# An attention and FFN block on one core: four groups of narrow value products, issued in two places or in four

## The chip, the cores and the metric

The program runs on one core of a Trainium2 chip. The metric is the device time of one execution in microseconds (us). The kernel before takes 776.32 us (median of 3 runs, 775.79 to 776.37).

The names of the engines in the profile: PE is the matrix engine (TensorE), PEld its weight loads, DVE the vector engine, ACT the scalar engine, POOL the GpSimd, SP the engine that issues most DMAs.

## What is computed

The input x has 16 sequences of 256 tokens and 256 features; the context has the same shape. First an mLSTM style attention of 8 heads of 32 features (queries from the normalised x, keys and values both the context), then a feed-forward network with two hidden layers of 1024.

```
x = x + mlstm(layernorm(x), ctx, ctx)          # gates, running maxima, 8 heads
#   s_mat  = (q @ k.T / sqrt(32)) * exp(log_d - max(log_d))
#   h      = (s_mat @ v) / (max(|rowsum(s_mat)|, exp(-m)) + 5e-5), then rms norm and gain
u = layernorm(x)
h = silu((u @ w1.T) * s1) * ((u @ w2.T) * s2)  # 256 -> 1024, twice
h = gelu((h @ h1.T) * t1)                      # 1024 -> 1024
h = gelu((h @ h2.T) * t2)                      # 1024 -> 1024
x = x + (h @ w3.T) * s3                        # 1024 -> 256
```

## The kernel before

The 16 sequences are worked in 8 pairs of two (`PAIRS`, index i). A pair's 512 tokens are the moving side of the FFN's matmuls; features lie on partitions. Every FFN operand is held as a high part and a low part, so each product is two matmuls, one of `h_hi` and one of `h_lo`, both into one PSUM bank of `ps_f` (L1434 and L1435 in the first layer, L1468 and L1469 in the hidden layers, L1503 and L1504 in the last). A matmul with 512 moving columns of this kind is called a large one below.

The engines work a software pipeline that is written out by hand. While PE runs the FFN of pair i, it also runs, at fixed places between the FFN's matmuls, the attention of pair j = i + 1 and the first steps (transposes, gates) of pair g = i + 2. Each engine has one list of instructions in the order in which they are written, and semaphores tie the lists together. PE's list for one pair is written by `batch`:

- `swiglu` for m of 0 to 7 (8 large matmuls each), with `scores(j, 0)` after m = 4;
- `hidden_layer(i, 0, ...)`, the first hidden layer. It runs the output groups m = 0 and 1 side by side over k = 0 to 6, calling `between(k)` after each k (4 large matmuls), then k = 7 for both. Each later m is 8 large matmuls, a call of `within(m)`, 8 large matmuls, a call of `after(m)`. The hooks `after_2`, `within_2` and `between_2` hang on it. `scores(j, 1)` comes after m = 3, `make_state(j)` after m = 5;
- `hidden_layer(i, 1, ...)`, the second hidden layer, with `between_3`, `within_3` and `after_3`: `turn_z(g)` after k = 3, `gates(g)` after m = 2, `turn_z2(j)` and `turn_rows(g)` after m = 7;
- `project`, the last layer.

`values(j, t, b)` is the step in question: sequence b of the pair, token tile t (each of the two 128-token tiles). It multiplies the weighted scores (held in `decay`) by the values (`v_aug`). The weights of one such matmul are 128 rows by 32 columns, so a head's 128 tokens are done as 4 strips of 32 (`values_of_head`), and a call has 8 heads times 4 strips = 32 matmuls of 33 moving columns, into bank 2 + b of `ps_a`. Each of them has two records in the trace. Such matmuls are called narrow ones below. `make_state` (L1371) has 16 of the same kind; `scores` (L1356) has 16 with 32 rows of weights; `read_state` (L1407) has 4 with the full 128 by 128.

What hangs on the values: after tile 0 of both sequences ACT copies them to `num` (`take_near`, L656, placed in ACT's list behind the group m = 5 of the first hidden layer), and only then may tile 1 be written to the same banks (`s_near`). After tile 1 of both, DVE adds the far part (`take_num`, L955, placed in DVE's list behind the last low part of the first hidden layer, L1076), and goes on from there through the division, the rms norm, the residual and the second layer norm. DVE's list then leads to the gates' scans of pair g, whose last step (L894) PE waits for in `turn_rows` (L1336). SP's load of the next values (L341) waits for the last values group too.

The pair after next uses the same code; there are 7 pairs i with an attention stage.

Of the kernel before, what the change touches and what calls it, by code (L numbers as in the profile page):

```python
# [73 lines left out]
def build(nc, x, ctx_tok, ctx_t, gate_w, gate_b, outnorm_w, w_cols, scales, w3_s, out):  # L74
    with ExitStack() as stack:
# [167 lines left out]
        def first(j):  # L243
            return isinstance(j, int) and j == 0
# [61 lines left out]
        def weights_in(eng, layer):  # L306
            eng.wait_ge(s_wgt[layer], 16 * sum(n == layer for n, _ in LOADS))
# [934 lines left out]
        def _(pe):  # L1242
# [6 lines left out]
            def turn_z(j):  # L1249
                pe.wait_ge(s_z, j)  # L1250

                if j >= 2:
                    pe.wait_ge(s_num, j)
                else:
                    pe.wait_ge(s_far, j)
                turn(z, ps_a[:, 0:CH], s_zT)
# [10 lines left out]
            def turn_z2(j):  # L1267
                pe.wait_ge(s_z2, j)
                if isinstance(j, int) and 0 < j < PAIRS - 1:

                    pe.wait_ge(s_zhi, j)
                turn(z2, ps_a[:, 0:CH], s_z2T)
# [60 lines left out]
            def turn_rows(j):  # L1333
                pe.wait_ge(s_scan, SCAN_STEPS * j + SCAN_STEPS)
                for t in range(TILES):
                    last = pe.transpose(rows_out[:, t * ROWS:(t + 1) * ROWS], rows[:, t * P:(t + 1) * P], ident[0:ROWS, 0:ROWS])  # L1336
                last.then_inc(s_colT, 1)

            def scores(j, b):
                if b == 0:  # L1340

                    pe.wait_ge(s_zTe, j + 1)
                    pe.wait_ge(s_cols, j + 1)
                    reuse(pe, s_z2lo, j)
                    reuse(pe, s_num, j)
                elif first(j):
                    pe.wait_ge(s_exp, EXP_STEPS)
                else:
                    pe.wait_ge(s_smat, SMAT_STEPS * j + ROWGRP)
                for t in range(TILES):  # L1350
                    for c in range(CH):
                        for r in range(ROWGRP):
                            d = slice(r * DH, (r + 1) * DH)
                            col = (c * TILES + t) * P
                            at = slice((b * TILES + t) * P, (b * TILES + t + 1) * P)
                            last = pe.matmul(score_out(j, b, r)[:, col:col + P], ctxT(j)[d, c, at], zT(j)[d, c, at], start=True, stop=True)  # L1356
                last.then_inc(s_qk, 1)

            def make_state(j):
                pe.wait_ge(s_kwt, j + 1)  # L1360
                pe.wait_ge(s_smat, SMAT_STEPS * j + (ROWGRP if first(j) else SMAT_STEPS))
                for b in range(W):
                    if first(j):
                        for c in range(CH):
                            h = slice(c * ROWGRP, (c + 1) * ROWGRP)
                            last = pe.matmul(ps_a[:, b, c * ROWGRP * DV:(c + 1) * ROWGRP * DV], k_wt[:, b, h, :],
                                             v_aug[:, b * TILES, h, :], start=True, stop=True)
                        continue
                    for h in range(HEADS):
                        strip = slice(h % ROWGRP * DH, (h % ROWGRP + 1) * DH)  # L1370
                        last = pe.matmul(ps_a[strip, b, h * DV:(h + 1) * DV], k_wt[:, b, h, :],  # L1371
                                         v_aug[:, b * TILES, h, :], start=True, stop=True)
                last.then_inc(s_st, 1)

            def values_of_head(j, b, h, t):

                for n in range(STRIPS):
                    strip = slice(n * STRIP, (n + 1) * STRIP)
                    last = pe.matmul(value_out(j, b, t)[strip, h * DV:(h + 1) * DV], decay_of(b, h, t)[:, strip],  # L1379
                                     v_aug[:, b * TILES + t, h, :], start=True, stop=True)  # L1380
                return last
# [11 lines left out]
            def values(j, t, b):  # L1393
                if t == 1:

                    pe.wait_ge(s_near, j + 1)
                for h in range(HEADS):
                    last = values_of_head(j, b, h, t)
                last.then_inc(s_pv, 1)
# [21 lines left out]
            def swiglu(i, m, as_is):  # L1421
                bank = (turn_of(i) + 2 * m) % 4
                if m == 1:

                    reuse(pe, s_ysc, W * i)
                if m >= 2:
                    pe.wait_ge(s_hf, KH * i + m - 1)
                per = KH // N_W1
                for half, base in enumerate((UNIT_W1, UNIT_W2)):
                    if as_is and m % per == 0:  # L1430
                        pe.wait_ge(*unit_landed(i - PAIRS, base + m // per))
                    for c in range(CH):
                        w = columns(base + m // per, (m % per * CH + c) * P, P, as_is)
                        pe.matmul(ps_f[:, bank + half], w, moving(z2_hi[:, c], as_is), start=(c == 0), stop=False)  # L1434
                        last = pe.matmul(ps_f[:, bank + half], w, moving(z2_lo[:, c], as_is), start=False, stop=(c == CH - 1))  # L1435
                last.then_inc(s_ab, 1)

            def first_swiglu():

                for part, landed in ((z2_hi, (s_z2hi_first, s_z2hi)), (z2_lo, (s_z2lo_first, s_z2lo))):  # L1440
                    for c in range(CH):
                        pe.wait_ge(landed[c], 1)
                        for half, base in enumerate((UNIT_W1, UNIT_W2)):
                            last = pe.matmul(ps_f[:, half], columns(base, c * P, P, False), part[:, c],
                                             start=(part is z2_hi and c == 0), stop=(part is z2_lo and c == CH - 1))
                last.then_inc(s_ab, 1)
# [75 lines left out]
            def count_inexact():  # L1522

                pe.wait_ge(s_inexact_sum, 1)
                pe.matmul(ps_a[0:1, 0, 0:1], inexact_sum[:], ones[:], start=True, stop=True).then_inc(s_inexact_all, 1)

            def batch(i, a_stage, g_stage, as_is=False, last=False):
                j, g = i + 1, i + 2
                if as_is:
                    pe.wait_ge(s_y, W * i)  # L1530
                weights_in(pe, 0)
                if not first(i):
                    pe.wait_ge(s_z2lo, i + 1)
                if first(i):
                    first_swiglu()
                for m in range(1 if first(i) else 0, KH):
                    swiglu(i, m, as_is)
                    if first(i) and m == 2:
                        turn_rows(1)
                    if a_stage and m == 4:  # L1540
                        scores(j, 0)

                def after_2(m):
                    if a_stage and m == 3:
                        scores(j, 1)
                    if a_stage and m == 5:
                        make_state(j)
                        values(j, 0, 0)
                        values(j, 0, 1)

                def after_3(m):
                    if g_stage and m == 2:
                        gates(g)
                    if a_stage and m == 7:
                        turn_z2(j)
                    if g_stage and m == 7:
                        turn_rows(g)

                def within_2(m):
                    if a_stage and m == 7:  # L1560
                        read_state(j)
                        values(j, 1, 0)
                        values(j, 1, 1)

                def between_2(k):
                    pass

                def between_3(k):
                    if g_stage and k == 3:
                        turn_z(g)  # L1570

                def within_3(m):
                    pass

                weights_in(pe, 1)
                hidden_layer(i, 0, as_is, between_2, within_2, after_2)
                weights_in(pe, 2)
                hidden_layer(i, 1, as_is, between_3, within_3, after_3)
                weights_in(pe, 3)
                project(i, as_is, last)  # L1580
                if last:
                    count_inexact()
# [97 lines left out]
```

## Time and profile before

| | |
|---|---|
| median of 3 runs | 776.32 us |
| the profiled execution | 775.79 us |
| its span, first to last instruction | 773.9 us |
| mean granted clock of TensorE | 0.996 |
| PE busy | 764.5 us |
| DVE busy | 545.8 us |
| ACT busy | 381.6 us |
| POOL busy | 50.9 us |

The span and the engines' times are of one profiled execution. Between the span and that execution's own time lie 1.9 us. A busy share says how long an engine had an instruction under way; large matmuls overlap, so the distance between the starts of two of them is shorter than the duration of one.

### The profile page before, as it was taken

How to read it: one execution, taken by the hardware profiler on the slowest of the kernel's cores; microseconds unless marked ns; L12 is line 12 of the kernel's file. 1: busy time of each engine (PE TensorE's matmuls, PEld its weight loads, DVE VectorE, ACT ScalarE, POOL GpSimd, SP SyncE). 2: the span in 40 equal slices, each digit the busy share in tenths (PEclk: the TensorE clock that was granted, in tenths of full speed). 3: DMA queues.
4: the chain of work that ended last, by engine and by line, in shares of the span. 5: the costliest groups of instructions: out<-in, count | busy, mean ns of one | idle time of the engine just before them, and what ended most of it. 6: DMA issues, size and time to landing. Idle time of an engine off the chain costs nothing.

```text
span 773.9 us, 14930 instructions
## 1 busy us (share of the span) xinstructions
PE 764.5 (99%) x6170; PEld 640.6 (83%) x6170; DVE 545.8 (71%) x1294; ACT 381.6 (49%) x570; POOL 50.9 (7%) x63
## 2 busy tenths in 40 slices
PE   8999999999999999999999999999999999999997
PEld 7878888878888888878888888888889788888886
DVE  6787867586856969578675877758695684965544
ACT  3455645464554733556445564636435562445331
POOL 3300020000200011000200002000020000000000
PEclk9999999999999999999999999999999999999999
DMA  8933010501122000320005000130102100541540
GB/s 338 368 124 115 29 30 28 191 1 35 52 100 92 28 30 27 122 71 29 30 28 189 2 30 29 69 151 9 50 29 110 54 1 3 185 142 29 162 137 29
DMA packets 14615, 63.43 MB, mean 82 GB/s; under 512 B 2016, under 2 KB 2896, under 8 KB 11728
## 3 DMA queue, kind: packets, MB, share of 16 engines
q1 hardware_dynamic: 12960, 50.12, 18.7%
q0 software_dynamic: 1296, 11.53, 3.8%
q8 instruction: 49, 0.80, 0.4%
q10 hardware_dynamic: 288, 0.79, 0.3%
q14 instruction: 22, 0.18, 0.1%
HBM read 53.94 MB, written 8.50 MB: 81 GB/s over the span
## 4 chain that ended last, share of the span: by engine, by line
PE 85%; DVE 11%; ACT 2%; issue 1%; POOL 0%; POOLq 0%; DVEq 0%; ACTq 0%
PE ps_f L1468 24%; PE ps_f L1469 23%; DVE decay L917 8%; PE ps_f L1434 8%; PE ps_f L1435 7%; PE ps_f L1503 4%; PE ps_f L1504 4%; PE ps_a L1356 2%; PE ps_a L1379 2%; DVE decay L933 2%; PE ps_a L1246 2%; PE ps_f L1587 1%; PE ps_a L1282 1%; PE ps_f L1302 1%; PE ps_a L1407 1%
## 5 line engine op out<-in xcount | busy, mean ns | idle before, releaser
L1468 PE MATMUL ps_f<-h_hi,wgt 128*128 128x512 f32 x1024 | 401.7, 392 | 0.0
L1469 PE MATMUL ps_f<-h_lo,wgt 128*128 128x512 f32 x1024 | 398.8, 389 | 0.0
L1468 PEld LDWEIGHTS ps_f<-h_hi,wgt 128*128 128x128 f32 x1024 | 192.2, 188 | 41.6 <-issue 0.6
L1469 PEld LDWEIGHTS ps_f<-h_lo,wgt 128*128 128x128 f32 x1024 | 192.3, 188 | 38.8
L691 ACT ACTIVATE work<-ps_f,scl 128x512 f32<-128x512 f32 x128 | 87.5, 684 | 161.2 <-PE ps_f L1469 160.6
L1076 DVE TENSOR_TENSOR h_lo<-work,h_hi 128x512 fp32r<-128x512 f32 x128 | 86.5, 689 | 98.2 <-ACT h_hi L696 97.1
L1434 PE MATMUL ps_f<-h_hi,wgt 128*128 128x512 f32 x252 | 99.8, 396 | 0.0
L1435 PE MATMUL ps_f<-h_lo,wgt 128*128 128x512 f32 x252 | 98.7, 392 | 0.0
L678 ACT ACTIVATE work<-ps_f,scl 128x512 f32<-128x512 f32 x64 | 44.1, 689 | 98.2 <-PE ps_f L1435 96.3
L696 ACT ACTIVATE h_hi<-work 128x512 fp32r<-128x512 f32 x128 | 81.0, 633 | 4.1
L1067 DVE SCALAR_TENSOR_TENSOR work<-ps_f,scl,work 128x512 f32<-128x512 f32 x64 | 48.0, 750 | 47.0 <-ACT work L678 47.0
L917 DVE SCALAR_TENSOR_TENSOR decay<-decay,cols,future 128x128 f32<-128x128 f32 x224 | 64.5, 362 | 0.0
L1503 PE MATMUL ps_f<-wgt,h_hi 128*128 128x256 f32 x256 | 62.3, 285 | 0.0
L1504 PE MATMUL ps_f<-wgt,h_lo 128*128 128x256 f32 x256 | 61.7, 283 | 0.0
L1434 PEld LDWEIGHTS ps_f<-h_hi,wgt 128*128 128x128 f32 x252 | 47.3, 188 | 14.7 <-DVE work L1067 3.8
L1435 PEld LDWEIGHTS ps_f<-h_lo,wgt 128*128 128x128 f32 x252 | 47.4, 188 | 8.6
L1504 PEld LDWEIGHTS ps_f<-wgt,h_lo 128*128 128x128 f32 x256 | 49.1, 192 | 0.0
L1503 PEld LDWEIGHTS ps_f<-wgt,h_hi 128*128 128x128 f32 x256 | 49.0, 192 | 0.0
L621 ACT ACTIVATE decay<-decay 128x1024 f32<-128x1024 f32 x28 | 29.7, 1061 | 35.3 <-DVE decay L917 35.3
L1072 DVE TENSOR_TENSOR h_lo<-work,h_hi 128x512 fp32r<-128x512 f32 x64 | 43.7, 682 | 0.8
L682 ACT ACTIVATE h_hi<-work 128x512 fp32r<-128x512 f32 x64 | 39.9, 623 | 2.4 <-DVE work L1067 2.4
L933 DVE SCALAR_TENSOR_TENSOR decay<-ps_a,decay 128x512 f32<-128x512 f32 x60 | 37.1, 677 | 0.7 <-PE ps_a L1356 0.7
(195 smaller groups left out, 701.1 us busy)
## 6 DMA issues: line engine op xcount, KB each, us to landing
decay<-m_rows SPq DMA_DIRECT2D x14, 1024.0 KB, 6.1
decay<-w_cols SPq DMA_DIRECT2D x22, 512.0 KB, 4.2
wgt<-w_cols POOLq DMA_DIRECT2D x5, 1024.0 KB, 11.8
v_aug<-ctx_tok SPq DMA_DIRECT2D x8, 528.0 KB, 4.0
wgt<-w_cols POOLq DMA_DIRECT2D x2, 2048.0 KB, 14.4
x_kept<-xs SPq DMA_DIRECT2D x8, 512.0 KB, 2.6
xs<-x SPq DMA_DIRECT2D x7, 512.0 KB, 3.6
ctxT<-ctx_t SPq DMA_DIRECT2D x7, 512.0 KB, 3.3
```

The costliest lines, as they stand in the source:

```text
L691: act.activation(work[:, m % GELU], ps_f[:, (turn_of(i) + m) % 4], ACT.Gelu, scale=scl[:, 2 + layer, m:m + 1]).then_inc(s_gelu, 1)
L696: act.activation(h_hi[1 - layer][:, m], work[:, m % GELU], ACT.Copy).then_inc(s_hi, 1)
L917: last = dve.scalar_tensor_tensor(part, part, cols[:, t, row:row + 1], future[:], ALU.subtract, ALU.add)
L933: dve.scalar_tensor_tensor(s, score_out(j, b, r).rearrange("p (c n) -> p c n", c=CH), SCORE_SCALE, s, ALU.mult, ALU.mult)\
L1067: dve.scalar_tensor_tensor(work[:, 2 + m % 2], ps_f[:, bank], scl[:, 1, m:m + 1], work[:, m % 2], ALU.mult, ALU.mult).then_inc(s_hf, 1)
L1076: dve.tensor_tensor(h_lo[1 - layer][:, m], work[:, m % GELU], h_hi[1 - layer][:, m].bitcast(F32), ALU.subtract).then_inc(s_lo, 1)
L1434: pe.matmul(ps_f[:, bank + half], w, moving(z2_hi[:, c], as_is), start=(c == 0), stop=False)
L1435: last = pe.matmul(ps_f[:, bank + half], w, moving(z2_lo[:, c], as_is), start=False, stop=(c == CH - 1))
L1468: pe.matmul(ps_f[:, bank], w, moving(h_hi[layer][:, k], as_is), start=(k == 0), stop=False)
L1469: last = pe.matmul(ps_f[:, bank], w, moving(h_lo[layer][:, k], as_is), start=False, stop=(k == KH - 1))
L1503: pe.matmul(to, moving(h_hi[0][:, k, q * P:(q + 1) * P], as_is), w, start=(k == 0), stop=False)
L1504: last = pe.matmul(to, moving(h_lo[0][:, k, q * P:(q + 1) * P], as_is), w, start=False, stop=(k == KH - 1))
```

## The change

Two of the four calls of `values` for a pair move. `values(j, 0, 1)` goes from directly behind `values(j, 0, 0)` to 8 large matmuls later, the middle of the group m = 6. `values(j, 1, 1)` goes from directly behind `values(j, 1, 0)` to behind the remaining 8 large matmuls of m = 7 and the first 4 of the second hidden layer. No instruction is added or taken away, and the lists of DVE, ACT, POOL and SP stay as they are.

```diff
                     if a_stage and m == 5:
                         make_state(j)
                         values(j, 0, 0)
-                        values(j, 0, 1)
...
                 def within_2(m):
+                    if a_stage and m == 6:
+                        values(j, 0, 1)
                     if a_stage and m == 7:
                         read_state(j)
                         values(j, 1, 0)
-                        values(j, 1, 1)
...
                 def between_3(k):
+                    if a_stage and k == 0:
+                        values(j, 1, 1)
                     if g_stage and k == 3:
                         turn_z(g)
```

PE's list behind the group m = 5 of the first hidden layer, before. Rows are line, operation, result and operands, tile size, a count, and the semaphores waited for.

```order
L1371 MATMUL ps_a<-v_aug,num 32x33 [waits s_smat,s_kwt]
L1371 MATMUL ps_a<-v_aug,num 32x33 x15
L1379 MATMUL ps_a<-v_aug,decay 32x33 x64
L1468 MATMUL ps_f<-h_hi,wgt 128x512 [waits s_gelu]
L1469 MATMUL ps_f<-h_lo,wgt 128x512
```

The same place with the change:

```order
L1371 MATMUL ps_a<-v_aug,num 32x33 x15
L1379 MATMUL ps_a<-v_aug,decay 32x33 x32
L1468 MATMUL ps_f<-h_hi,wgt 128x512 [waits s_gelu]
L1469 MATMUL ps_f<-h_lo,wgt 128x512
L1468 MATMUL ps_f<-h_hi,wgt 128x512
L1469 MATMUL ps_f<-h_lo,wgt 128x512
L1468 MATMUL ps_f<-h_hi,wgt 128x512
L1469 MATMUL ps_f<-h_lo,wgt 128x512
L1468 MATMUL ps_f<-h_hi,wgt 128x512
L1469 MATMUL ps_f<-h_lo,wgt 128x512
L1379 MATMUL ps_a<-v_aug,decay 32x33 x32
L1468 MATMUL ps_f<-h_hi,wgt 128x512
```

The 64 narrow matmuls of tile 0 now stand as 32 and 32, with 8 large ones between them.

PE's list in the middle of the group m = 7, before; the second hidden layer begins behind 8 large matmuls, at the row that waits for `s_lo`, `s_gelu` and `s_wgt2`:

```order
L1407 MATMUL ps_a<-state,zT 128x132 x3
L1379 MATMUL ps_a<-v_aug,decay 32x33 [waits s_near]
L1379 MATMUL ps_a<-v_aug,decay 32x33 x31
L1379 MATMUL ps_a<-v_aug,decay 32x33 [waits s_near]
L1379 MATMUL ps_a<-v_aug,decay 32x33 x31
L1468 MATMUL ps_f<-h_hi,wgt 128x512
L1469 MATMUL ps_f<-h_lo,wgt 128x512
```

With the change, the end of the first hidden layer and the start of the second:

```order
L1469 MATMUL ps_f<-h_lo,wgt 128x512
L1468 MATMUL ps_f<-h_hi,wgt 128x512 [waits s_lo,s_gelu,s_wgt2]
L1469 MATMUL ps_f<-h_lo,wgt 128x512
L1468 MATMUL ps_f<-h_hi,wgt 128x512 [waits s_lo,s_gelu]
L1469 MATMUL ps_f<-h_lo,wgt 128x512
L1379 MATMUL ps_a<-v_aug,decay 32x33 [waits s_near]
L1379 MATMUL ps_a<-v_aug,decay 32x33 x31
L1468 MATMUL ps_f<-h_hi,wgt 128x512 [waits s_lo]
```

Tile 1 of the second sequence now runs inside the second hidden layer, behind that layer's first 4 large matmuls.

## Rows read from the trace of the kernel before

**Rows 1.** The page: busy time of each engine, and the granted clock by slice.

```profile
PE 764.5 (99%) x6170; PEld 640.6 (83%) x6170; DVE 545.8 (71%) x1294; ACT 381.6 (49%) x570; POOL 50.9 (7%) x63
...
PEclk9999999999999999999999999999999999999999
```

**Rows 2.** Busy time by window, one pair: busy, records, clock, DMA share, GB/s.

```profile
191.00:282.00 91.00, 90.90 (x777) 76.28 (x765) 66.39 (x161) 47.61 (x69) 6.23 (x4) 1.00 0.17 59
```

**Rows 3.** Timeline of PE behind m = 5: start us, length us, line, shapes, count.

```profile
273.28 0.39 PE L1469 MATMUL ps_f<-h_lo,wgt 128*128 128x512 f32 x1
273.60 0.46 PE L1371 MATMUL ps_a<-v_aug,num 128*32 128x33 f32 x32
273.88 1.34 PE L1379 MATMUL ps_a<-v_aug,decay 128*32 128x33 f32 x128
275.15 0.50 PE L1468 MATMUL ps_f<-h_hi,wgt 128*128 128x512 f32 x1
275.48 0.39 PE L1469 MATMUL ps_f<-h_lo,wgt 128*128 128x512 f32 x1
...
276.87 0.39 PE L1469 MATMUL ps_f<-h_lo,wgt 128*128 128x512 f32 x1
```

**Rows 4.** Timeline of PE in the middle of m = 7, same pair.

```profile
280.50 0.39 PE L1469 MATMUL ps_f<-h_lo,wgt 128*128 128x512 f32 x1
280.72 1.06 PE L1407 MATMUL ps_a<-state,zT 128*128 128x132 f32 x8
281.71 1.32 PE L1379 MATMUL ps_a<-v_aug,decay 128*32 128x33 f32 x128
282.97 0.50 PE L1468 MATMUL ps_f<-h_hi,wgt 128*128 128x512 f32 x1
283.30 0.40 PE L1469 MATMUL ps_f<-h_lo,wgt 128*128 128x512 f32 x1
...
285.61 0.39 PE L1469 MATMUL ps_f<-h_lo,wgt 128*128 128x512 f32 x1
```

**Rows 5.** All narrow matmuls of the values: duration ns min/median/max, starts.

```profile
L1379 PE MATMUL ps_a<-v_aug,decay x1792: 192/197/218, 91.4 to 647.9; 128*32 128x33 f32 x200
```

**Rows 6.** Timeline of PE around the first scores of a pair.

```profile
243.19 0.39 PE L1435 MATMUL ps_f<-h_lo,wgt 128*128 128x512 f32 x1
243.51 1.17 PE L1356 MATMUL ps_a<-zT,ctxT 32*128 32x128 f32 x32
244.61 0.50 PE L1434 MATMUL ps_f<-h_hi,wgt 128*128 128x512 f32 x1
244.95 0.40 PE L1435 MATMUL ps_f<-h_lo,wgt 128*128 128x512 f32 x1
```

**Rows 7.** Timeline of PE around the transposes of `turn_z`.

```profile
288.56 1.03 PE L1246 MATMUL ps_a<-ident,z 128*128 128x128 f32 x8
289.35 0.48 PE L1468 MATMUL ps_f<-h_hi,wgt 128*128 128x512 f32 x1
289.67 0.40 PE L1469 MATMUL ps_f<-h_lo,wgt 128*128 128x512 f32 x1
```

**Rows 8.** Timelines of DVE and ACT: the takers of the values.

```profile
286.51 0.69 DVE L1076 TENSOR_TENSOR h_lo<-work,h_hi 128x512 fp32r<-128x512 f32 x1 [3.98 <-ACT h_hi L696]
287.12 0.70 DVE L955 TENSOR_TENSOR num<-ps_a,state 128x528 f32<-128x528 f32 x1
...
275.25 0.61 ACT L656 ACTIVATE num<-ps_a 128x528 f32<-128x528 f32 x1 [0.19 <-PE ps_a L1379]
```

**Rows 9.** Timelines of DVE and PE: scans' end, and `turn_rows`.

```profile
316.43 0.27 DVE L894 TENSOR_SCALAR rows<-state 16x128 f32<-16x128 f32 x1
...
317.60 0.30 PE L1336 MATMUL ps_a<-ident,rows 80*128 80x80 f32 x2
```

**Rows 10.** Waits of PE's weight loads: us in total, times, longest.

```profile
PEld ps_a L1356 <- DVE decay L933: 3.7, 7, 0.5
```

## The prediction

> **What bounds the kernel now.** I read the busy times first: PE has work under way for 764.5 of 773.9 us, DVE for 545.8, ACT for 381.6, and every slice of the granted clock shows a 9, the top digit [rows 1]. Then a window of one pair: 90.90 of 91.00 us busy at a granted clock of 1.00, that is 2.4 GHz, with the DMA engines at 0.17 [rows 2]. So from the first pair to the last PE's own list sets the end: what PE's stream gains or loses in length, the kernel gains or loses, unless a wait appears. The only wait on another engine that returns in every pair is at the second scores, 3.7 us over 7 times [rows 10]; its cause, the masks on DVE, starts from the first FFN layer of the same pair, which the change does not touch, so it moves along with PE.
>
> Busy shares don't tell what a change of order costs, since matmuls overlap. That is read from the starts of neighbouring matmuls on the timeline. Undisturbed large ones are 0.227 us apart: from 276.87 [rows 3] to 280.50 [rows 4] there are 16 distances in 3.63 us.
>
> **What a run of narrow matmuls costs at its edges.** At the first place [rows 3]:
> - Entry: from the start of the last large matmul, 273.28, to the first narrow one, 273.60, is 0.32 us and not 0.227: 0.09 more.
> - Exit: the run of 128 records ends at 273.88 + 1.34 = 275.22; one of them takes 0.197 [rows 5], so the last one starts at 275.02, and the large one behind it at 275.15: 0.13. Within the run the starts are (275.02 - 273.88) / 127 = 0.009 apart, so 0.12 is due to the exit.
> - Aftermath: the first large matmul lasts 0.50, its neighbour starts 0.33 behind it, and the 8th large one starts at 276.87. Seven distances take 1.72 us where 7 x 0.227 = 1.59: 0.13 more.
>
> Together 0.09 + 0.12 + 0.13 = 0.34 us at the edges of a run, whatever is in it. At the second place [rows 4] the aftermath over the 12 large matmuls from 282.97 to 285.61 is 2.64 - 11 x 0.227 = 0.14, and the exit from 281.71 + 1.32 - 0.197 = 282.83 to 282.97 is 0.14 - 0.01 = 0.13; with an entry of 0.09, 0.36 us. Are these edges of a size that depends on the length of the run? The scores, a run of 32 records, show the same three signs [rows 6]: 0.32 from 243.19 to 243.51, 0.50 for the first large one, 0.34 to the next. So a run a quarter as long pays the same.
>
> **The change, part by part.** Nothing is added or removed: the 896 narrow matmuls of the values stand in the new list too, with their 1.1 to 1.3 us per 128 records. What changes is the number of runs. Before, a pair has two runs with values in them; now it has four. The first run keeps the state and 64 records, then come 8 large matmuls, then 64 records on their own; the second keeps the read of the state and 64 records, then 12 large ones, then 64 records. In 8 large matmuls the aftermath of [rows 3] is over (from 276.87 on the distances are 0.227), so neither new piece shares its edges with the old. Each new run costs one full set of edges:
>
> 2 runs x 7 pairs x 0.35 us (the mean of 0.34 and 0.36) = 4.9 us. The start of a fresh run looks a little quicker than its middle (32 records of the state in 0.28 us [rows 3], 8.8 ns each, against 9.0), a gain of 64 x 0.2 ns = 0.01 per run: 0.1 us. The sum is 4.8 us.
>
> What hides it? Nothing that I find: PE has no slack to lay it in. What other engines do with the moved times:
> - ACT copies tile 0 at 275.25, as soon as the last narrow one is done [rows 8]. The last narrow matmul of tile 0 comes later by the 8 large ones plus one set of edges, 1.8 + 0.34 = 2.2 us, so the copy lies at about 277.4 to 278.0. Its reader on PE starts at 281.71 [rows 4]: over 3 us of cover. Queued behind the copy on ACT is the group m = 6, which PE ends 8 large matmuls (1.8 us) after the values, later than a copy of 0.61 us: nobody waits for it.
> - DVE takes the values of tile 1 at 287.12, directly behind the last low part [rows 8]. The last large matmul of m = 7 starts 64 records sooner against its run (0.57 us) and one set of edges later, so this low part and `take_num` come about 0.23 sooner, at 286.9. The values of tile 1 then lie behind the 4th large matmul of the next layer. Before, that layer began 8 large ones behind 282.97 with the aftermath, at 284.93 (282.97 + 8 x 0.227 + 0.14); now it begins at 284.93 - 0.57 + 0.34 = 284.70, the run starts 3 x 0.227 + 0.32 later, at 285.70, its last record starts at 286.26 and ends at 286.46. DVE would be there at 286.9: 0.4 us to spare. This is the closest call of the change.
> - SP's load of the next values waits for the last narrow matmul, which comes some 3.4 us later. Its reader is in the next pair's stretch, and behind it in SP's list stands a wait for the residual of the same pair, which comes later still. Cost: nothing.
>
> **A rule of the skill.** The trace shows the entry and exit gaps of 0.09 and 0.12 where the weights go from 128 columns to 32 and back [rows 3], and none at the entry of the read of the state, whose weights are as wide as the large ones': 280.50 to 280.72 is the usual distance [rows 4]. The Trainium skill, page "TensorEngine Tiling (Array Packing)", section "Key Properties", says that changing the tiling mode, not just the tile, drains the engine, which speaks against this change. By that rule alone each new run has two drains and no aftermath, and the sum would be 14 x (0.09 + 0.12) = 2.9 us. The trace agrees on the two gaps and shows the aftermath on top.
>
> **Bounds.** The new runs of 64 records with nothing ahead of them have no exact row. From below: the transposes, with weights of full width, have an aftermath as well, 0.32 from 289.35 to 289.67 [rows 7], 0.09 in that distance alone; entry plus that is 0.18 per run, 2.6 us in all. From above: 0.36 plus a further 0.08, the entry's size once more, should the new place in the second layer, where two accumulations are open, cost an extra gap: 14 x 0.44 = 6.2 us. I take 0.35, since the two rows it comes from are the same instructions at the same places.
>
> **Rivals.**
> 1. The values of tile 1 become late for DVE. From `take_num` on DVE is busy without a gap into the scans, whose end at 316.43 + 0.27 = 316.70 PE reads at 317.60 in `turn_rows` [rows 9]: 0.9 us of slack, and with the change PE comes there another 0.9 us later against DVE (64 records and a set of edges now lie between). It decides from a lateness of 0.4 + 1.8 = 2.2 us on; a run of 0.57 us would have to take 2.8. If the lateness came to 3 us, 6 pairs would pay 0.8 us each: 4.8 + 4.8 = 9.6 us, some 786 us. Against it: the 197 ns of each narrow matmul vary only from 192 to 218 [rows 5].
> 2. Not slower. The edges belong to the length of the run: a short run is drained while the large matmuls' weights are already loaded, and only the last run of a place pays. Then each split costs little, and half-length runs could cost up to their entry, 14 x 0.09 = 1.3 us, or with a free entry 0; and if DVE, whose list is then shifted against PE's, came earlier to the masks, the waits of [rows 10] could go as well, 3.7 us less. That is 772.6 to 777.6 us. For it: the long runs here are the only ones with 128 records. Against it: the 32 records of the scores pay the same edges [rows 6], and the masks follow the first FFN layer of their own pair, by when all that moved is long past. It decides from the point where the edges of a 64-record run come to under 0.11 us together (1.6 us in 14).
> 3. Two drains and no aftermath, as worked out above: 2.9 us, about 779.2 us, slower still.
>
> **How the numbers follow.** The sum stands against the profiled execution: 775.79 + 4.8 = 780.6 us; its span would be 773.9 + 4.8 = 778.7. That execution was 0.5 us below the median of its three, so the median to expect is 776.32 + 4.8 = 781.1. I say 781.0. Chances: the forecast with a full set of edges (3.8 to 6.2 us more) 0.73; rival 3 and what lies between it and the forecast (2.6 to 3.8) 0.16; rival 1 0.04; rival 2 0.07. The range reaches down to rival 3's 776.32 + 2.9 = 779.2 and up to 776.32 + 6.2 = 782.5; it holds the forecast and most of rival 3, some 0.84. Within 0.2% is 1.6 us either way, about what a measurement of this kernel tells from no change: slower 0.93 (the forecast and rivals 3 and 1), same 0.05 and faster 0.02, both from rival 2.
>
> **What would show it.** On PE's timeline behind m = 5 there should be two runs, each entered 0.32 behind a large start, each left with a large matmul of 0.50 and a distance of 0.33; the middle of m = 7 and the start of the next layer alike. The distance between the same place of two pairs should grow by 0.7 us. `take_num` should still follow the last low part at once, and the PE waits should be what they are. PE's busy total should grow little, since gaps of this kind hide in overlapping records. I am wrong if a run of 64 records shows no entry gap or no aftermath, if the distance of pairs grows by less than 0.3 us, or if `turn_rows` or `turn_z` starts to wait.

## The result and the profile after

The changed kernel takes 781.33 us (median of 4 runs, 781.02 to 781.58) where the kernel before takes 776.09 (median of 4, 775.79 to 776.37). The ratio is 1.0066, its 95% interval 1.0055 to 1.0079: slower by 4.3 to 6.1 us, in the middle 5.1. The profiled execution took 780.64 us with a span of 778.9, 5.0 more than the 773.9 of before.

The busy times of the changed kernel, against [rows 1]:

```profile
PE 769.4 (99%) x6170; PEld 641.0 (82%) x6170; DVE 551.4 (71%) x1294; ACT 381.8 (49%) x570; POOL 50.8 (7%) x63
...
PEclk9999999999999999999999999999999999999999
```

The records are as many as before and the clock is as high. PE has grown by 4.9 us, the whole difference, and DVE by 5.6. The prediction foresaw neither: it expected PE's total to grow little.

PE's timeline at the first place, start and length in us, against [rows 3]:

```profile
274.75 0.39 PE L1469 MATMUL ps_f<-h_lo,wgt 128*128 128x512 f32 x1
275.07 0.46 PE L1371 MATMUL ps_a<-v_aug,num 128*32 128x33 f32 x32
275.35 0.78 PE L1379 MATMUL ps_a<-v_aug,decay 128*32 128x33 f32 x64
276.06 0.50 PE L1468 MATMUL ps_f<-h_hi,wgt 128*128 128x512 f32 x1
276.39 0.40 PE L1469 MATMUL ps_f<-h_lo,wgt 128*128 128x512 f32 x1
...
277.76 0.39 PE L1469 MATMUL ps_f<-h_lo,wgt 128*128 128x512 f32 x1
278.08 0.76 PE L1379 MATMUL ps_a<-v_aug,decay 128*32 128x33 f32 x64
278.78 0.50 PE L1468 MATMUL ps_f<-h_hi,wgt 128*128 128x512 f32 x1
279.12 0.40 PE L1469 MATMUL ps_f<-h_lo,wgt 128*128 128x512 f32 x1
```

Both runs have the three edges: 0.32 us from the last large start to the first narrow one (274.75 to 275.07, and 277.76 to 278.08), a large matmul of 0.50 behind them, and 0.33 or 0.34 to the next. The new run takes 278.78 - 278.08 = 0.70 us from its first narrow start to the large one behind it, half of what 128 records take in [rows 3] plus an exit. In the second hidden layer the new run looks alike:

```profile
286.88 0.39 PE L1469 MATMUL ps_f<-h_lo,wgt 128*128 128x512 f32 x1
287.20 0.77 PE L1379 MATMUL ps_a<-v_aug,decay 128*32 128x33 f32 x64
287.90 0.50 PE L1468 MATMUL ps_f<-h_hi,wgt 128*128 128x512 f32 x1
```

A number that runs through all that follows is the distance between the same place of two neighbouring pairs. Here it is read from the start of the state's run (L1371). First the kernel before (its next one is in [rows 3], at 273.60), then the changed one (its next one is above, at 275.07):

```profile
182.37 0.46 PE L1371 MATMUL ps_a<-v_aug,num 128*32 128x33 f32 x32
```

```profile
183.10 0.46 PE L1371 MATMUL ps_a<-v_aug,num 128*32 128x33 f32 x32
```

That is 91.23 us before and 91.97 now: 0.74 per pair. For a table of all kernels I took the distances between the first large matmul of neighbouring pairs (the first of `swiglu`, L1434 in the kernel before) from the timelines, from the second pair on, and of the first five of them the middle one. The edits of the others follow below. The ratios are against executions of the kernel before that ran beside the kernel in question (their medians are 776.2 to 776.4 us), and a difference in us further down is worked out from the ratio. Medians and ratios leave out the few executions that ran in a slower state (946.54 us for one with joined transposes, 825.63 for one of the full width, together, 844.31 and 2692.4 for two of the kernel before).

| kernel | distance of pairs, us | against before | time, us (median) | ratio to before (95%) |
|---|---|---|---|---|
| before | 91.25 | | 776.09 | |
| changed | 91.97 | +0.72 | 781.33 | 1.0066 (1.0055 to 1.0079) |
| tile 0 split alone | 91.66 | +0.41 | 778.71 | 1.0032 (1.0019 to 1.0044) |
| tile 1 split alone | 91.70 | +0.45 | 778.61 | 1.0031 (1.0019 to 1.0042) |
| tile 0 split by 2 large | 91.62 | +0.37 | 778.59 | 1.0028 (1.0018 to 1.0037) |
| tile 0 in four runs | 92.30 | +1.05 | 783.44 | 1.0092 (1.0077 to 1.0108) |
| changed, tile 1 later | 92.00 | +0.75 | 781.39 | 1.0065 (1.0051 to 1.0078) |
| full width, together | 95.77 | +4.52 | 809.74 | 1.0466 (1.0434 to 1.0498) |
| full width, split | 95.85 | +4.60 | 808.16 | 1.0412 (1.0398 to 1.0425) |
| later scores | 92.03 | +0.78 | 781.80 | 1.0067 (1.0054 to 1.0080) |
| later scores, joined transposes | 93.40 | +2.15 | 789.67 | 1.0170 (1.0157 to 1.0184) |
| joined transposes | 92.63 | +1.38 | 784.77 | 1.0111 (1.0093 to 1.0129) |
| floors later | 91.13 | -0.12 | 775.10 | 0.9988 (0.9979 to 0.9997) |
| floors later, joined | 92.43 | +1.18 | 783.08 | 1.0093 (1.0078 to 1.0109) |

### The profile page after: what moved, and what is told of

Read it like the earlier page. It is cut to its first block, busy times and chain, and to the rows that moved or that the text cites. A ratio compares the mean times of both kernels' runs of the same rounds, so it can differ in the third digit from the quotient of the medians.

```text
span 778.9 us, 14930 instructions
## 1 busy us (share of the span) xinstructions
PE 769.4 (99%) x6170; PEld 641.0 (82%) x6170; DVE 551.4 (71%) x1294; ACT 381.8 (49%) x570; POOL 50.8 (7%) x63
## 4 chain that ended last, share of the span: by engine, by line
PE 84%; DVE 13%; ACT 2%; issue 1%; POOL 0%; DVEq 0%; POOLq 0%; ACTq 0%
PE ps_f L1468 24%; PE ps_f L1469 23%; DVE decay L917 8%; PE ps_f L1434 8%; PE ps_f L1435 7%; PE ps_f L1503 4%; PE ps_f L1504 4%; PE ps_a L1379 2%; PE ps_a L1356 2%; DVE decay L933 2%; PE ps_a L1246 1%; PE ps_f L1302 1%; PE ps_a L1407 1%; PE ps_a L1329 1%; PE ps_a L1322 1%
## 5 line engine op out<-in xcount | busy, mean ns | idle before, releaser
L1469 PE MATMUL ps_f<-h_lo,wgt 128*128 128x512 f32 x1024 | 398.9, 390 | 0.0
L1469 PEld LDWEIGHTS ps_f<-h_lo,wgt 128*128 128x128 f32 x1024 | 192.3, 188 | 38.4
L1434 PE MATMUL ps_f<-h_hi,wgt 128*128 128x512 f32 x252 | 99.8, 396 | 0.0
L1434 PEld LDWEIGHTS ps_f<-h_hi,wgt 128*128 128x128 f32 x252 | 47.3, 188 | 14.6 <-DVE work L1067 3.4
```

The source lines that it names most:

```text
L1469: last = pe.matmul(ps_f[:, bank], w, moving(h_lo[layer][:, k], as_is), start=False, stop=(k == KH - 1))
```

## The experiments

### Is it the number of runs, and which half pays?

Theory: each separate run of narrow matmuls costs its edges. The rivals: the values of tile 1 are late for DVE, or the length of a run decides. Two kernels make half of the change each.

```diff
                         values(j, 0, 0)
-                        values(j, 0, 1)
...
                 def within_2(m):
+                    if a_stage and m == 6:
+                        values(j, 0, 1)
```

> Only tile 0 is split: values(j,0,1) moves behind the first 8 large matmuls of m = 6; tile 1 stays together. Theory of the edges (each separate run of narrow matmuls costs entry 0.09, exit 0.12 and aftermath 0.13 us, whatever is in it): 7 more runs, 7 x 0.34 = 2.4 us over before, half of the change. Rival, length of the run decides (a run of 64 records pays little, the long ones much): under 1 us. Rival, lateness of the values for DVE is what costs in the changed kernel: 0 here, since tile 1 is not moved and ACT's copy has over 3 us to spare.

Measured: 778.71 us, ratio 1.0032, that is 2.5 us more.

```diff
                         values(j, 1, 0)
-                        values(j, 1, 1)
...
                 def between_3(k):
+                    if a_stage and k == 0:
+                        values(j, 1, 1)
```

> Only tile 1 is split: values(j,1,1) moves behind the first 4 large matmuls of the second hidden layer; tile 0 stays together. Theory of the edges: 7 more runs, 2.4 to 2.5 us over before, and with the kernel that splits tile 0 alone it adds up to the whole change. Rival, lateness: the whole of the change's 5 us sits here. Rival, length: under 1 us.

Measured: 778.61 us, ratio 1.0031, 2.4 us more. Each half pays half, so the cost goes with the number of runs and not with the one that stands nearest to a reader. By the times the halves add up to the whole, 4.9 us against 5.1. By the pair distances they are 0.41 and 0.45, and the whole is 0.72 and not 0.86; steps of 0.03 us, by which these timelines differ at places that no edit touched too, make up a part of that, and whether the rest belongs to the edges is not shown. The single distances behind a run vary by some hundredths from kernel to kernel; a rule for it I did not find.

Next, tile 0 in four runs of 32 records, 2, 6 and 8 large matmuls apart.

```diff
                     if a_stage and m == 5:
                         make_state(j)
-                        values(j, 0, 0)
-                        values(j, 0, 1)
+                        values(j, 0, 0, range(4))
+                    if a_stage and m == 6:
+                        values(j, 0, 1, range(4, 8))
...
                 def within_2(m):
+                    if a_stage and m == 6:
+                        values(j, 0, 1, range(4))
...
+                def soon_2(m):
+                    if a_stage and m == 6:
+                        values(j, 0, 0, range(4, 8))
```

> Tile 0's values in four runs instead of one: 4 heads (32 records) behind make_state, then 2 large matmuls, 4 heads, 6 large, 4 heads, 8 large, 4 heads. Three more runs per pair than before, each of half the changed kernel's length. If a run costs its edges whatever its length: 3 x 7 x 0.34 to 0.4 = 7.1 to 8.4 us over before, pairs 1.0 to 1.2 us further apart. If what a run costs grows with its length, 32 records should pay about half of what 64 pay: 4 us.

Measured: 783.44 us, 7.1 us more, 1.05 per pair, 0.35 for each of the three added runs. PE's timeline of this kernel (its large matmuls are L1469 and L1470) around the second and third run:

```profile
277.59 0.46 PE L1379 MATMUL ps_a<-v_aug,decay 128*32 128x33 f32 x32
277.99 0.50 PE L1469 MATMUL ps_f<-h_hi,wgt 128*128 128x512 f32 x1
278.33 0.40 PE L1470 MATMUL ps_f<-h_lo,wgt 128*128 128x512 f32 x1
...
279.27 0.39 PE L1470 MATMUL ps_f<-h_lo,wgt 128*128 128x512 f32 x1
279.59 0.46 PE L1379 MATMUL ps_a<-v_aug,decay 128*32 128x33 f32 x32
279.98 0.50 PE L1469 MATMUL ps_f<-h_hi,wgt 128*128 128x512 f32 x1
```

Thirty-two records take 0.40 us up to the next large start, and then the same 0.50 and 0.34 follow as behind 128. The price is per run, not per record: this is the plainest evidence against rival 2 of the prediction.

Last of this group, tile 0 split with only 2 large matmuls between.

```diff
                         make_state(j)
                         values(j, 0, 0)
-                        values(j, 0, 1)
...
+                def soon_2(m):
+                    if a_stage and m == 6:
+                        values(j, 0, 1)
...
                 for m in range(2, KH):
+                    if layer == 0 and m >= 6:
+                        hidden(i, layer, m, range(1), as_is)
+                        soon(m)
```

> Only tile 0 is split, with 2 large matmuls between its two runs instead of 8. The aftermath of a run is a distance of 0.33 to the second large matmul and then about 0.02 spread over the next six. If the edges belong to the switch itself, nearly the full price is paid: entry 0.09, exit 0.12, aftermath 0.11, so 0.32 x 7 = 2.2 us over before. If the aftermath is a debt of the run just ended that two large matmuls cannot pay and that is paid once at the end, 0.2 x 7 = 1.5 us. If the time depends on how long narrow work runs without a break, something near 0.

Measured: 778.59 us, ratio 1.0028, 2.2 us. Its pair distance is 0.04 less than with 8 large matmuls between. So two large matmuls are enough for nearly the full price, and the long first distance is most of the aftermath.

### How late may the values of tile 1 be?

This edit is against the changed kernel: tile 1 of the second sequence goes behind 12 large matmuls of the second hidden layer instead of 4.

```diff
                 def between_3(k):
-                    if a_stage and k == 0:
+                    if a_stage and k == 2:
                         values(j, 1, 1)
```

> The changed kernel, with values(j,1,1) behind 12 instead of 4 large matmuls of the second hidden layer, 8 x 0.227 = 1.8 us later. DVE then comes to take_num before the values are there and waits about 1.4 us in every pair. Theory of the edges with slack behind DVE of about 2.2 us (up to the scans that turn_rows waits for): the same time as the changed kernel, within 0.5 us, although DVE waits. Rival, DVE's chain is already at its limit in the changed kernel: 6 or 7 x 1.4 = 8 to 10 us slower than the changed kernel.

Measured: 781.39 us, the changed kernel's time. DVE does wait, as DVE's timeline shows:

```profile
289.95 0.71 DVE L955 TENSOR_TENSOR num<-ps_a,state 128x528 f32<-128x528 f32 x1 [1.41 <-PE ps_a L1379]
290.75 0.56 DVE L1009 SCALAR_TENSOR_TENSOR den<-num 128x32 f32<-128x32 f32 x1
```

A new wait of 1.41 us in every pair costs nothing, though not for the reason forecast. The operation behind it, L1009, takes 0.56 us here; in the kernels before and after it takes 2.04 to 2.07. It ends at 291.31, where it ended at 291.26 in the changed kernel: the wait was laid into a stretch that was lost already. What loses it comes below.

### Do the edges belong to the narrow weights?

Both kernels do a head's values as one matmul with full-width weights, in the order of before and of the change.

```diff
-                for n in range(STRIPS):
-                    strip = slice(n * STRIP, (n + 1) * STRIP)
-                    last = pe.matmul(value_out(j, b, t)[strip, h * DV:(h + 1) * DV], decay_of(b, h, t)[:, strip],
-                                     v_aug[:, b * TILES + t, h, :], start=True, stop=True)
-                return last
+                return pe.matmul(value_out(j, b, t)[:, h * DV:(h + 1) * DV], decay_of(b, h, t),
+                                 v_aug[:, b * TILES + t, h, :], start=True, stop=True)
```

> The kernel before, with each head's values done as one matmul with weights of 128 by 128 instead of 4 with weights of 128 by 32: the array's division into column strips is gone from the values. The first pair's values (L1389 of before) run so, 0.112 us from record to record, so 2 runs of 32 records x 0.112 = 3.6 us take the place of 128 x 0.009 = 1.1: about 5 us per pair, 34 us in all. It is the partner of the run in which these are split.

> The changed kernel with the same full-width values. What counts is the difference to its partner in which they stay together. If the edges come from the change between full weights and column strips, entry (0.09) and exit (0.12) go, and what is left is what the transposes show at theirs, 0.09 per run: 14 x 0.09 = 1.3 us. If any short foreign run between the large matmuls pays the edges, the difference is the change's, 4.8 us. If neither, 0.

Measured, by pair distances: 95.77 together, 95.85 split. The same two extra runs that cost 0.72 us per pair with narrow weights cost 0.08 with wide ones, 0.6 us in all where 1.3 were expected. A new run of the split kernel, with the large matmul ahead (L1466) and behind (L1465):

```profile
286.70 0.39 PE L1466 MATMUL ps_f<-h_lo,wgt 128*128 128x512 f32 x1
286.93 1.87 PE L1377 MATMUL ps_a<-v_aug,decay 128*128 128x33 f32 x16
288.63 0.48 PE L1465 MATMUL ps_f<-h_hi,wgt 128*128 128x512 f32 x1
288.95 0.40 PE L1466 MATMUL ps_f<-h_lo,wgt 128*128 128x512 f32 x1
```

The entry gap is gone (0.23 from 286.70 to 286.93), the exit too (sixteen records at 0.112 would reach 288.72, and the large one starts at 288.63); only the 0.32 behind the first large matmul stays. That alone would be 0.09 for each new run; most of it comes back inside the runs: the new one takes 1.70 us from its first start to the large one behind it, and the one of 32 records that it was taken from is shorter by 1.79. So the entry and the exit come with the change between full weights and 32-column strips. The Trainium skill's page "TensorEngine Tiling (Array Packing)", section "Key Properties", says that a change of the tiling mode drains the engine; these rows agree. A part of the aftermath, 0.09, comes without that change as well, here and behind the transposes of [rows 7].

The medians of the two stand the other way round, 809.74 and 808.16, and this I had not expected. The profiled execution of the joined kernel shows what adds to its time, in its timeline from the first pair:

```profile
91.58 3.76 PE L1377 MATMUL ps_a<-v_aug,decay 128*128 128x33 f32 x32
95.17 0.48 PE L1465 MATMUL ps_f<-h_hi,wgt 128*128 128x512 f32 x1
...
95.75 0.63 PE L1465 MATMUL ps_f<-h_hi,wgt 128*128 128x512 f32 x1
```

and in its busy times by window (window, its length, busy time and records of PE, PEld, DVE, ACT and POOL, then the granted clock, the DMA share and GB/s):

```profile
90.00:95.00 5.00, 5.00 (x69) 4.49 (x67) 4.52 (x22) 1.32 (x2) 0.00 (x0) 1.00 0.00 0
95.70:99.00 3.30, 3.30 (x9) 2.58 (x8) 1.10 (x2) 0.28 (x1) 0.00 (x0) 0.50 0.00 0
```

Right behind a run of 4 us of full-width matmuls with only 33 moving columns, the clock falls from its 2.4 GHz level to 1.2 GHz and large matmuls take 0.63 us. PE was busy all that time, 5.00 of 5.00 us. In this execution it happened behind one of the 14 such runs, and that pair is 1.7 us longer than the others. The six executions range from 808.94 us at a mean granted clock of 0.995 to 825.63 at 0.975, and the longer ones are those with the lower clock; that they have more such falls is the likely reason, but only the 808.94 one has a trace. Split into runs of at most 2.6 us the same work keeps 0.996 or 0.997 and stays within 807.89 to 808.35. So there is a case in which splitting helps. Among the pairs of the kernel before it does not arise: the granted clock is 1.00 from 50 to 700 us, and their runs of small matmuls last 2.3 us at most. Ahead of the first pair it does, in that kernel as in both with full-width weights, where the values of the first pair run with full-width weights (L1389, 33.94 to 37.59 in the kernel before). Its busy times by window, during that run and behind it:

```profile
33.90:37.40 3.50, 3.50 (x34) 3.50 (x34) 2.52 (x4) 0.00 (x0) 0.00 (x0) 1.00 1.02 421
38.00:40.00 2.00, 2.00 (x9) 1.38 (x8) 1.80 (x6) 1.27 (x3) 0.00 (x0) 0.50 1.07 430
```

In the kernel with the later scores the same run is followed by a clock of 1.00, so such a run is not followed by a fall each time.

### Fewer or better placed runs

If a run costs its edges, a kernel with fewer waits and runs should be faster than before. Two edits to the order of before, and both together:

```diff
                 def after_2(m):
-                    if a_stage and m == 3:
-                        scores(j, 1)
...
                 def within_2(m):
+                    if a_stage and m == 4:
+                        scores(j, 1)
```

> The kernel before with scores(j,1) moved from behind m = 3 to the middle of m = 4 of the first hidden layer, 8 large matmuls (1.8 us) later. No run is added. PE's wait of 0.17 us beyond the entry in each pair (0.49 us between the starts at 264.53 and 265.02 where an entry takes 0.32) goes, and DVE's weighing of these scores starts at 268.06 behind a low part, after the scores would be done at about 267.9: 7 x 0.17 = 1.2 us faster than before. Rival, the runs' places cost, not their number: anything else; slower if DVE now waits for the scores and passes it on.

Measured: 781.80 us, 5.2 us slower, a clear miss. PE's timeline of this kernel:

```profile
266.71 0.39 PE L1469 MATMUL ps_f<-h_lo,wgt 128*128 128x512 f32 x1
267.78 0.50 PE L1468 MATMUL ps_f<-h_hi,wgt 128*128 128x512 f32 x1 [0.68 <-ACT work L691]
```

ACT's timeline at the same place:

```profile
264.67 1.06 ACT L621 ACTIVATE decay<-decay 128x1024 f32<-128x1024 f32 x1 [1.04 <-DVE decay L917]
265.74 1.28 ACT L691 ACT_TABLE_LOAD   x1
267.04 0.69 ACT L691 ACTIVATE work<-ps_f,scl 128x512 f32<-128x512 f32 x1
```

The large matmul of m = 4 reuses the bank of m = 0 and needs ACT's first gelu, which stands behind the exponentials and a table load. In the kernel before the scores fill that hole with 1.1 us of PE work. Moving them took away a wait of 0.17 us and laid bare one of about 0.84 (from 266.71 to 267.78, less 0.227), which makes 0.67 of the 0.78 by which the pairs grew. The expectation had looked at DVE behind the scores and not at ACT.

The next edit joins `turn_z(g)` to the values of tile 1. The transposes then stand ahead of `take_num`, so their wait for `s_num` has to go, too. The kernel with both edits was run first, and the one with the joined transposes alone was made to split its loss.

```diff
-                if j >= 2:
-                    pe.wait_ge(s_num, j)
-                else:
-                    pe.wait_ge(s_far, j)
+                pe.wait_ge(s_far, j)
...
                         values(j, 1, 1)
+                    if g_stage and m == 7:
+                        turn_z(g)
...
                 def between_3(k):
-                    if g_stage and k == 3:
-                        turn_z(g)
```

> The kernel before with turn_z(g) behind the values of tile 1 in the same run, and nothing else. Edges alone: the transposes' aftermath of 0.09 us and something of the narrow run's go in 6 pairs, 0.6 to 0.8 us faster. But PE then reaches turn_rows 0.8 + 0.1 us sooner against DVE's chain from take_num to the scans, and there it had 0.9 us of slack. If that slack is what limits, turn_rows begins to wait by about 0.1 to 0.2 us per pair, and the time is that of before or up to 0.5 us more, not the 13 us of the kernel that has the later scores too.

> As the one with the later scores, and turn_z(g) joined to the run of tile 1's values (L1246 directly behind L1379, no large matmuls between) instead of a run of its own in the second hidden layer. Theory of the edges: the transposes' own aftermath of 0.09 us goes in 6 pairs, 0.6 us, and up to 0.13 - 0.09 more where the aftermath of full-width work replaces that of narrow work: together 1.8 to 2.1 us faster than before. Rival, the transposes wait for the far part on DVE (s_far): each 0.1 us of it takes 0.6 us away, and the sum is 1.2 us or less.

Measured: 784.77 us with the joined transposes alone, 8.6 more than before, and 789.67 with both, 13.2 more. Both are misses: a gain was expected of both edits together (1.8 to 2.1 us, or 1.2 by the rival), and at most 0.5 us more for the one. PE's waits on other engines in the kernel with the joined transposes alone (us in total, times, longest; L1333 is `turn_rows` there):

```profile
PE ps_a L1333 <- DVE rows L894: 7.2, 6, 1.2
```

`turn_rows` waits 1.2 us in six pairs, at least six times what was expected. The wait is where rival 1 of the prediction put it. PE's earlier arrival uses up the 0.9 us of slack, as expected, but the 1.2 us on top are not explained by PE's order. DVE's timeline behind `take_num` shows the rest:

```profile
292.18 2.08 DVE L1009 SCALAR_TENSOR_TENSOR den<-num 128x32 f32<-128x32 f32 x1
294.29 2.29 DVE L1010 SCALAR_TENSOR_TENSOR den<-den,floor 128x32 f32<-128x32 f32 x1
```

and POOL's timeline of the same kernel:

```profile
291.77 2.41 POOL L507 TENSOR_TENSOR h_lo<-ctxT,h_hi 128x1024 fp32r<-128x1024 f32 x1 [32.67 <-ACT h_hi L561]
294.13 2.40 POOL L511 TENSOR_TENSOR h_lo<-zT,h_hi 128x1024 fp32r<-128x1024 f32 x1
```

Two DVE operations on 32 elements per partition, about 0.2 us elsewhere, end within 0.1 us behind POOL's operations, however long those still run. In the kernel before L1010 takes 0.19 and L1020 is the one that is held, for 1.03; here L1010 loses 2.10 us and L1020 wins 0.84, since POOL's second operation, which waits for ACT's copy of these transposes, has moved up. DVE's chain is 1.3 us longer. The Trainium skill, page "GPSIMD Engine Reference", section "1. Specifications", says that GpSimd shares its SBUF interfaces with VectorE, with contention where the DVE instruction is in a 2-port perf mode or has two SBUF inputs. L1009, L1010 and L1020 have two, and these rows agree. One operation with a single SBUF input was held as well, L1022 in the kernel with full-width weights, split, usually 0.18 us; which mode it ran in no run here shows. DVE's row, then POOL's:

```profile
305.56 2.33 DVE L1022 TENSOR_SCALAR rms<-rms 128x32 f32<-128x32 f32 x1
```

```profile
305.46 2.40 POOL L511 TENSOR_TENSOR h_lo<-zT,h_hi 128x1024 fp32r<-128x1024 f32 x1 [3.59 <-ACT h_hi L578]
```

The last edit leaves PE's list alone: on DVE the two small operations of `floors` go behind the weighing of the first scores. It was tried by itself and together with the joined transposes.

```diff
                     masks(j)
-                    floors(j)
                     weigh_scores(j, 0)
+                    floors(j)
```

> The kernel before, PE's list untouched; on DVE the two small operations of floors (L925, 0.23 us in all) stand behind the weighing of the first scores instead of ahead of it. The weighing then ends about 0.15 us sooner, and PE's wait at the second scores, 0.17 us beyond the entry, shrinks to 0.02: 7 x 0.15 = 1.0 us faster. The large matmul behind these scores needs the first gelu of the hidden layer (ACT, 264.82 + 0.69 = 265.51) and would start at 265.97, so 0.4 us remain there. Rival, PE is held by ACT at that place, as in the kernel with the later scores: no change.

Measured: 775.10 us, ratio 0.9988 (0.9979 to 0.9997). The pairs are 0.12 us closer. On PE's timeline the entry into the second scores goes from 0.49 (264.53 to 265.02, the first two rows, of the kernel before) to 0.36 (the last two, of this one):

```profile
264.53 0.39 PE L1469 MATMUL ps_f<-h_lo,wgt 128*128 128x512 f32 x1
265.02 1.17 PE L1356 MATMUL ps_a<-zT,ctxT 32*128 32x128 f32 x32
```

```profile
264.83 0.39 PE L1469 MATMUL ps_f<-h_lo,wgt 128*128 128x512 f32 x1
265.19 1.17 PE L1356 MATMUL ps_a<-zT,ctxT 32*128 32x128 f32 x32
```

This is the one edit that beats the kernel before, by about 0.9 us (0.2 to 1.6), and it doesn't touch PE's list.

> Both of the last two edits. If the pair's length is set by PE alone, the gains add: 1.6 us faster. If with the joined transposes it is DVE's chain between take_num and the scans that PE waits for, what is won at the second scores stays won, since that chain starts behind it: again the sum of the two.

Measured: 783.08 us, 7.2 more than before, where 1.6 less was expected. Against the joined transposes alone it is 0.20 us per pair, so what the floors win is kept, but neither edit turns the other into a gain.

## Why the prediction was right

**The bound.** PE's list sets the end in both kernels: its distance between pairs grew by 0.72 us, 7 pairs make 5.0 us, and the span grew by 5.0.

**The term.** 14 runs at 0.35 us, less 0.1, made 4.8 us against the profiled execution; it measured 4.85 (780.64 - 775.79), and 5.2 between the medians. Entry 0.32 was right to the last digit, the exit 0.13 for the 0.12 expected, and the first distance behind it 0.33 or 0.34. With the starts of the large matmuls of both kernels laid side by side over one pair, the first new run cost 0.40 us and the second 0.34, where 0.35 was taken for each. The prediction tied entry and exit to the width of the weights by two single rows; the kernels with full-width weights bear that out.

**The cover.** DVE was forecast to come to `take_num` 0.23 us sooner and to find the values with 0.4 us to spare. The rows of the changed kernel:

```profile
287.79 0.69 DVE L1076 TENSOR_TENSOR h_lo<-work,h_hi 128x512 fp32r<-128x512 f32 x1 [3.41 <-ACT h_hi L696]
288.40 0.70 DVE L955 TENSOR_TENSOR num<-ps_a,state 128x528 f32<-128x528 f32 x1
...
294.42 1.87 DVE L1020 TENSOR_TENSOR rms<-rms,den 128x32 f32<-128x32 f32 x1
```

The last record of the values ends at 287.20 + 0.77 = 287.97, 0.43 before `take_num` at 288.40, without a wait. Counted from the start of the pair, `take_num` came 0.18 us sooner. ACT's copy came 2.17 us later where 2.2 was forecast, and nobody waited for it.

**What was wrong in it.** "PE's busy total should grow little, since gaps of this kind hide in overlapping records" came out the other way: it grew by 4.9 us, the whole cost. The records overlap over the gaps, so the gaps count as busy time, and a longer list of the same instructions shows in full in the total. The wait at the second scores was also not the only one that returns in every pair. This row of the kernel before has two or three waits per pair:

```profile
PEld ps_f L1434 <- DVE work L1067: 3.8, 21, 0.3
```

With the change it is 3.4 us over 19 waits, so nothing of the difference lies there. In rival 1 I let the slack at `turn_rows` grow from 0.9 to 1.8 us, because 0.9 us of PE's work now lies between. It stayed where it was, 319.79 - (318.59 + 0.27) = 0.93 us in the changed kernel:

```profile
318.59 0.27 DVE L894 TENSOR_SCALAR rows<-state 16x128 f32<-16x128 f32 x1
...
319.79 0.30 PE L1336 MATMUL ps_a<-ident,rows 80*128 80x80 f32 x2
```

PE's gain was eaten on DVE, where L1020 went from 1.03 to 1.87 us, since POOL's second operation waits for the transposes behind the moved values, comes 0.9 us later against `take_num` (before 291.65 - 287.12 = 4.53, now 293.85 - 288.40 = 5.45) and holds L1020 longer. POOL's rows, before and with the change:

```profile
291.65 2.44 POOL L511 TENSOR_TENSOR h_lo<-zT,h_hi 128x1024 fp32r<-128x1024 f32 x1 [1.77 <-ACT h_hi L578]
```

```profile
293.85 2.40 POOL L511 TENSOR_TENSOR h_lo<-zT,h_hi 128x1024 fp32r<-128x1024 f32 x1 [2.66 <-ACT h_hi L578]
```

Six pairs of 0.84 us are 5.0 of the 5.6 us by which DVE's busy time grew. It cost nothing here; in the kernels with joined transposes the same effect cost 1.3 us per pair. The point from which rival 1 would decide was therefore about 1.3 us of lateness for an unchanged POOL, not 2.2, and yet a wait of 1.41 was free in the kernel with the later tile 1, because L1009 ends with POOL's operation in either case.

**The rivals.** Rival 2, that edges depend on the length of a run, fell with the four runs of 32 records, which paid 0.35 us each. Rival 3, two drains without aftermath, fell with the rows: the 0.33 behind the first large matmul is there every time.

## What to carry to other kernels

On a full PE, small matmuls with strips of weights should stand in as few runs as the dependencies allow: each run between large matmuls cost 0.35 us or so here, whether it had 32 records or 128. Where it is lost is read from the distances between neighbouring starts: the busy share is 99% in both kernels, since the gaps lie under overlapping records. Before a run is moved, look at what it hides for other engines as well (here an ACT table load behind the scores) and at which operations of POOL and DVE it brings together.

## What the runs showed of the hardware

- Entry into a run of narrow matmuls took 0.32 us between starts instead of 0.227, the exit 0.12 to 0.13 more, and the first large matmul behind it was followed after 0.33; with weights of full width only the last of the three (0.32) remained.
- The clock can fall from 2.4 to 1.2 GHz on a PE that is never idle: behind 4 us of full-width matmuls with 33 moving columns it was at 0.50 over 3.30 us, behind one of 14 such runs. The kernel before has such a fall too, ahead of its first pair, at 0.50 from 38 to 40 us with PE busy throughout.
- Small DVE operations with two SBUF inputs that began beside a running POOL operation ended with it: 0.19 us of work took up to 2.30. One with a single input did so too (L1022, 2.33), while another, L1019, took its usual 1.22 us beside POOL.
